# A quantiser's cube taken out of the last tiles' way, and a slot's largest value moved ahead of the late tables

## The chip, the cores and the metric

One core of a Trainium2 chip runs the whole program. It has TensorE (PE, matrix products, with weight loads shown apart as PEld), VectorE (DVE), ScalarE (ACT), GpSimd (POOL, which here also issues all indirect transfers) and SyncE (SP, which issues the direct ones). They meet only through semaphores. The metric is the device time of the program in microseconds (us). The kernel before takes 260.91 us, the median of three runs from 260.31 to 262.14.

## The reference

A sequence of 4 x 512 tokens of width 512 goes through two expert layers, each a residual on a layer norm. `route` stands for the choice of an expert per token:

```python
h = layernorm(x)                                     # layer 1: 4 experts, by token id
x = x + where(route, (silu(h @ C[e].T) * (h @ C[e].T)) @ C[e], 0)

h = layernorm(x)                                     # layer 2: 8 experts, by argmax(h @ router.T)
wq = clip(round(w * s), -1, 1) / s,      s = 1 / clip(mean|w|, 1e-5)
aq = clip(round(a * t), -128, 127) / t,  t = 127 / clip(max|a| over the row, 1e-5)
g, u = aq(h) @ wq(wg[e]).T, aq(h) @ wq(wu[e]).T
r = square(relu(g)) * u
x = x + where(route, aq(r) @ wq(wd[e]).T, 0)
```

All weights of layer 2 become ternary (-1, 0, 1), the activations 8-bit integers. A row's step is t8 = max(1, ratio)/127 in the kernel's scaled units; since r is a square times a linear term, the step enters the second quantiser as its **cube**.

## The kernel before, in words

**Layer 1** handles 19 tiles (B1) of 128 token rows, gathered in order of their expert by POOL's indirect transfer (L468). It goes through the loop over t: PE does two products per tile in split precision (L1484), transposes (L1470), and the router's logits (L1564). DVE writes the result row (L1047, function `residual`), its largest square (L1062, `largest`) and the row's index within its layer-2 expert (L1092, `row_index`). POOL works out the quantiser of the row (`deviation_of`, `roots_of`, `ratio_of`, `cube_of`, L497 to L533), the address (L542, `place`) and stores the 128 rows of 520 columns to DRAM at addresses sorted by expert (L550, `store`). Columns 512 to 519 carry the row's scalars: RSTD, INV, SCALE, NEG, TOKEN, CUBE.

**Layer 2** handles 23 slots (B2) of 128 rows, each of one expert. Slots 0 to 4 (EARLY) are blocks filled by tiles 0 to 14; they are loaded before the last tiles are done. Slots 5 to 22 are late: SP loads them (L391, `load`) once the last three stores have landed and the late tables are there (`slots_ready` at 2). The **late tables** (`late_slots`, `slot_tables`, `slot_factors`, a generator that DVE takes in steps with `next(late)`) say which rows and which expert each slot has: L1108, L1111, L1113, L1117, L1120 (`base`, the row address, signals `slots_ready`), L1125, L1129 (expert), L1137 to L1151 (means of the weights).

A slot takes these steps. DVE quantises the row (L1228, `quantise`), PE transposes it (L1586) and ACT copies it out (L745, qT); PE does the gate and up products (L1592); ACT takes relu and square (L753, L757); DVE multiplies (L1238, `product_of`), takes the largest value (L1248, `largest_product`), its reciprocal and the scale (L1256 and L1262, `product_scale`); ACT quantises the product (L777); PE transposes (L1586), ACT copies (L765), PE does the down product (L1592); DVE adds (L1283, `output`); POOL scatters the rows (L619, `scatter`). POOL also works out out_scale (L609) and, per group of slots, `factors_of`: cap_scale, down_size, least_max (L593 to L596) from the cubes in the loaded rows. `product_scale` waits until the whole group's factors are there (semaphore `sizes`). The late groups are slots 5 to 8, 9 and 10, 11 to 14, 15 to 18, 19 to 22; a group's factors are issued at step u = (first slot - 1), after all its rows have landed.

Every engine runs its instructions in the order written; no planner moves them. In a step u of layer 2 PE does gate(u), up(u), transpose q(u+1), transpose r(u-2), down(u-3); ACT relu and square of u, qT(u+1), rT(u-2), r8(u-1); DVE quantise(u+1), largest and scale of u-1, output(u-4), product(u). In step 4, DVE's quantise(5) stands ahead of product_of(3), and relu2(u) on ACT waits for product_of(u-1), which reads the same tile.

Of the kernel before, what the change touches and what calls it, by code (L numbers as in the profile page):

```python
# [5 lines left out]
ALU = mybir.AluOpType  # L6
ACT = mybir.ActivationFunctionType
X = mybir.AxisListType.X
F32 = mybir.dt.float32
# [4 lines left out]
I32 = mybir.dt.int32  # L14
U32 = mybir.dt.uint32

P = 128
# [20 lines left out]
ROW = D + 8  # L38
RSTD, INV, SCALE, NEG, TOKEN, CUBE = range(D, D + 6)

# [52 lines left out]
def moe_program(nc, x_in, tokens_in, ctx_in, router_in, weights_in, out):  # L93
    with ExitStack() as whole:
# [108 lines left out]
        by_slot = [sb("by_slot0", [P, 2 * EARLY], F32), sb("by_slot1", [P, 3 * (B2 - EARLY)], F32)]  # L203

        masked, late_token = sb("masked", [P, B2 - EARLY], I32), sb("late_token", [P, B2 - EARLY], I32)
        cap_scale, down_size = sb("cap_scale", [P, B2], F32), sb("down_size", [P, B2], F32)
# [133 lines left out]
        def sizes_of(group):  # L340

            return 3 * group

# [68 lines left out]
        def _(pool):  # L412
# [31 lines left out]
            for r in row:  # L444
                pool.memset(r[:, CUBE + 1:], 0.0).then_inc(made, 1)

# [53 lines left out]
            def steps_of(b):  # L500
                roots_of(b)
                ratio_of(b)
                cube_of(b)

            def roots_of(b):
                if not 0 <= b < B1:
                    return
                s, r = ln2[b % 2], row[b % ROWS]
                pool.wait_ge(norm2, 7 * b + 1)
                pool.wait_ge(largest_ready, b + 1)  # L510
                pool.tensor_tensor(r[:, RSTD:INV + 1], s[:, 2:4], half_powers[:, :], ALU.pow).then_inc(norm2, 1)  # L511
                pool.wait_ge(norm2, 7 * b + 3)
                pool.tensor_scalar(r[:, SCALE:SCALE + 1], r[:, INV:INV + 1], r[:, RSTD:RSTD + 1], QMAX,
                                   ALU.min, ALU.mult).then_inc(norm2, 1)

            def ratio_of(b):
                if not 0 <= b < B1:
                    return
                s, r = ln2[b % 2], row[b % ROWS]


                pool.wait_ge(norm2, 7 * b + 3)
                pool.tensor_scalar(s[:, 4:5], r[:, INV:INV + 1], s[:, 3:4], r[:, RSTD:RSTD + 1],
                                   ALU.mult, ALU.mult).then_inc(norm2, 1)

            def cube_of(b):
                if not 0 <= b < B1:
                    return
                s, r = ln2[b % 2], row[b % ROWS]
                pool.wait_ge(norm2, 7 * b + 5)  # L530
                pool.tensor_scalar(s[:, 4:5], s[:, 4:5], 1.0, 1.0 / QMAX, ALU.max, ALU.mult).then_inc(norm2, 1)
                pool.wait_ge(norm2, 7 * b + 6)
                pool.tensor_scalar(r[:, CUBE:CUBE + 1], s[:, 4:5], s[:, 4:5], s[:, 4:5],  # L533
                                   ALU.mult, ALU.mult).then_inc(norm2, 1)
# [10 lines left out]
            def store(b):  # L545
                if not 0 <= b < B1:
                    return
                pool.wait_ge(store_at_ready, b + 1)
                pool.wait_ge(norm2, 7 * b + 7)
                pool.indirect_dma_start(x1_rows, bass.IndirectOffsetOnAxis(ap=store_at[b % ROWS][:, :], axis=0),  # L550
# [18 lines left out]
            for t in range(TICKS):  # L569
                if t >= 2:  # L570
                    gather(t + 3)
                quantising(t - 2)
                place(t - 3)
                if t < B1:
                    store(t - 3)
                if t >= 2:
                    inverse_deviation(t + 2)

            def factors_of(group):
# [9 lines left out]
                if slots[0] == EARLY:  # L589

                    pool.tensor_scalar(masked[:, :], by_slot[1][:, 2 * n:3 * n], token1[:, 0:1], float(MASKED),
                                       ALU.is_ge, ALU.mult).then_inc(masked_ready, 1)
                pool.tensor_tensor(cap_scale[:, few, None], cols_of(slots, CUBE), gu, ALU.mult).then_inc(sizes, 1)  # L593
                pool.tensor_tensor(down_size[:, few, None], cols_of(slots, CUBE), gud, ALU.mult).then_inc(sizes, 1)
                pool.wait_ge(sizes, sizes_of(group - 1) + 1)
                pool.tensor_tensor(least_max[:, few], cap_scale[:, few], minus_one[:, few], ALU.pow).then_inc(sizes, 1)  # L596
                if late:
                    which = slice(slots[0] - EARLY, slots[-1] + 1 - EARLY)
                    pool.wait_ge(masked_ready, 1)
# [235 lines left out]
        def _(dve):  # L835
# [203 lines left out]
            def residual(b):  # L1039
# [3 lines left out]
                if b >= 2:  # L1043
                    dve.wait_ge(norm2, 7 * (b - 1))
                if b >= ROWS:
# [736 lines left out]
```

## Time and profile before

| | |
|---|---|
| profiled execution, time | 260.85 us |
| its span | 258.9 us |
| PE, DVE, ACT, POOL busy | 236.6, 219.7, 210.8, 164.9 us |
| granted TensorE clock, mean | 0.996 of 2.4 GHz |
| DMA | 51.71 MB, 200 GB/s mean |
| layer 1 | about 13 to 176 us |
| layer 2 | about 176 to 252 us |

A row's time is counted from the start of the span; 1.95 us of the execution's time lie outside the span. Busy time of an engine is no bound by itself: what counts is which wait ends last at each place, and whether PE, which has most work, stands still.

### The profile page before, as it was taken

What the parts mean: (1) busy time and instruction counts of PE and PEld (TensorE: products, weight loads), DVE (VectorE), ACT (ScalarE), POOL (GpSimd) and SP (SyncE); (2) the same over time, 40 slices, a digit from 0 to 9 for tenths busy, and PEclk for the clock granted to TensorE, in tenths of its full rate; (3) what the DMA queues carried; (4) which work ended last, traced back from release to release, by engine and by line L of the source; (5) the groups of instructions that cost most, each with busy time, mean ns of one, the idle gap of its engine ahead of it and who ended that gap; (6) DMA issues with size and microseconds to landing.
All of it is one profiled execution on the core that took longest, in us unless ns stands there. A gap on an engine that the chain in (4) does not pass through costs nothing.

```text
span 258.9 us, 5787 instructions
## 1 busy us (share of the span) xinstructions
PE 236.6 (91%) x1410; PEld 172.8 (67%) x1420; DVE 219.7 (85%) x686; ACT 210.8 (81%) x322; POOL 164.9 (64%) x322
## 2 busy tenths in 40 slices
PE   2388999999999999999999999989899999999970
PEld 2235678888888888888888888866355555555530
DVE  5969989979889988898888978869989999999861
ACT  1765799799889888898888888777799999999960
POOL 4463566768866867577676565558728675657553
PEclk9999999999999999999999999999999999999998
DMA  5969972946755599785577534551368962211110
GB/s 194 429 211 389 404 285 86 365 160 237 246 166 159 145 345 406 272 322 146 207 244 228 151 117 161 204 155 57 89 188 273 337 232 83 84 40 67 61 42 0
DMA packets 13726, 51.71 MB, mean 200 GB/s; under 512 B 2750, under 2 KB 2750, under 8 KB 10112
## 3 DMA queue, kind: packets, MB, share of 16 engines
q1 hardware_dynamic: 8816, 37.91, 42.3%
q0 software_dynamic: 4880, 13.44, 14.7%
q8 instruction: 14, 0.23, 0.4%
q14 instruction: 16, 0.13, 0.1%
HBM read 40.49 MB, written 13.48 MB: 208 GB/s over the span
## 4 chain that ended last, share of the span: by engine, by line
PE 79%; DVE 7%; DMA 7%; issue 4%; ACT 1%; POOL 1%; DVEq 0%; POOLq 0%; ACTq 0%
PE bank L1484 38%; PE bank L1592 20%; PE bank L1470 9%; PE bank L1564 6%; DMA staged<-weight_chunks 4%; PE bank L1586 4%; DMA x<-x_rows,gather 2%; PE bank L1503 1%; DVE ctx_lo L933 1%; POOL out_rows L619 1%; DMA token_ids<-token_ids_in 1%; PE bank L1459 1%; DVE at_least L853 1%; DVE stats L991 1%; DVE ternary L899 0%
## 5 line engine op out<-in xcount | busy, mean ns | idle before, releaser
L1592 PE MATMUL bank<-ternary,qT 128*128 x179 | 43.4, 379 | 0.9 <-ACT qT L745 0.5
L665 ACT ACTIVATE ternary<-staged 128x2048 bf16<-128x2048 f32 x20 | 38.0, 1899 | 2.0 <-DMA staged<-weight_chunks 2.0
L671 ACT ACTIVATE ternary<-staged,w_scale 128x1536 int16<-128x1536 f32 x20 | 31.5, 1575 | 2.2 <-DVE w_scale L947 0.6
L1592 PEld LDWEIGHTS bank<-ternary,qT 128*128 128x128 bf16 x184 | 17.7, 97 | 21.4 <-issue 5.9
L550 POOL DMA_INDIRECT x_rows<-row,store_at x19 | 22.2, 1166 | 14.9 <-POOL store_at L542 10.1
L619 POOL DMA_INDIRECT out_rows<-late_rows,late_token x18 | 19.7, 1095 | 16.1 <-DVE late_rows L1283 14.4
L468 POOL DMA_INDIRECT x<-x_rows,gather x16 | 19.1, 1193 | 9.6 <-issue 5.8
L718 ACT ACTIVATE p<-bank,rstd 128x512 f32<-128x512 f32 x19 | 13.0, 685 | 14.2 <-PE bank L1484 14.1
L1592 PE MATMUL bank<-ternary,rT 128*128 x87 | 22.7, 379 | 1.8 <-ACT rT L765 1.5
L1027 DVE SCALAR_TENSOR_TENSOR p<-bank,rstd,p 128x512 f32<-128x512 f32 x19 | 14.2, 749 | 10.5 <-ACT p L718 10.4
L1484 PE MATMUL bank<-ctx_hi,pT_hi 128*128 x76 | 22.4, 416 | 0.3 <-DVE pT_lo L1036 0.3
L1484 PE MATMUL bank<-ctx_hi,hT_hi 128*128 x76 | 22.3, 414 | 0.0
L1484 PE MATMUL bank<-ctx_lo,hT_hi 128*128 x76 | 21.0, 399 | 0.2 <-DVE ctx_lo L933 0.2
L1484 PE MATMUL bank<-ctx_hi,pT_lo 128*128 x76 | 20.8, 395 | 0.0
L1484 PE MATMUL bank<-ctx_lo,pT_hi 128*128 x76 | 20.8, 395 | 0.0
L1564 PEld LDWEIGHTS bank<-router,x1T 128*128 128x128 f32 x152 | 19.7, 191 | 1.5
L1484 PE MATMUL bank<-ctx_hi,hT_lo 128*128 x76 | 20.5, 391 | 0.0
L1564 PE MATMUL bank<-router,x1T 128*128 128x8 f32 x152 | 18.3, 246 | 0.0
L1238 DVE TENSOR_TENSOR prod<-bank,relu 128x512 f32<-128x512 f32 x23 | 15.8, 686 | 1.8 <-ACT relu L757 0.4
L777 ACT ACTIVATE r<-prod,fac 128x512 int16<-128x512 f32 x23 | 16.5, 719 | 0.7 <-DVE fac L1262 0.7
L511 POOL TENSOR_TENSOR row<-ln,half_powers 128x2 f32<-128x2 f32 x19 | 13.8, 725 | 5.0 <-DVE squares L1062 5.0
L1484 PEld LDWEIGHTS bank<-ctx_lo,hT_hi 128*128 128x128 f32 x76 | 14.3, 189 | 3.9 <-issue 0.6
(232 smaller groups left out, 661.9 us busy)
## 6 DMA issues: line engine op xcount, KB each, us to landing
staged<-weight_chunks SPq DMA_DIRECT2D x20, 1024.0 KB, 5.4
late_rows<-x_rows SPq DMA_DIRECT2D x18, 260.0 KB, 3.9
ternary<-ctx_chunks SPq DMA_DIRECT2D x4, 1024.0 KB, 8.2
ternary<-weight_chunks SPq DMA_DIRECT2D x4, 1024.0 KB, 9.4
x_rows<-filler SPq DMA_DIRECT2D x1, 2080.0 KB, 12.8
staged<-x_rows SPq DMA_DIRECT2D x5, 260.0 KB, 3.3
x_rows<-row,store_at POOLq DMA_INDIRECT x19, 5.7
out_rows<-late_rows,late_token POOLq DMA_INDIRECT x18
```

The lines of the kernel that those rows point to most:

```text
L468: pool.indirect_dma_start(x[b % RING], None, x_in, bass.IndirectOffsetOnAxis(ap=gather1[:, b:b + 1], axis=0), bounds_check=N - 1, oob_is_e ...
L550: pool.indirect_dma_start(x1_rows, bass.IndirectOffsetOnAxis(ap=store_at[b % ROWS][:, :], axis=0), row[b % ROWS][:, :], None, bounds_check ...
L619: pool.indirect_dma_start(out, bass.IndirectOffsetOnAxis(ap=token, axis=0), cols_of([b], 0, D), None, bounds_check=N - 1, oob_is_err=False)\
L665: nc.scalar.activation(ternary[:, m * K * D:(m + 1) * K * D], staged_of(i), ACT.Abs, accum_out=abs_sum[:, 2 * i:2 * i + 1]).then_inc(abs_r ...
L671: nc.scalar.activation(ternary[:, m * K * D + DVE_COLS:(m + 1) * K * D].bitcast(I16), staged_of(i)[:, DVE_COLS:], ACT.Copy, scale=w_scale[ ...
L777: nc.scalar.activation(r8[:, :], prod[b % 2][:, :], ACT.Copy, scale=fac[b % 2][:, 2:3])\
L1027: dve.scalar_tensor_tensor(p[:, :], a_ps[b % 2][:, :], rstd1[b % 2][:, :], p[:, :], ALU.mult, ALU.mult).then_inc(p_ready, 1)
L1238: dve.tensor_tensor(prod[b % 2][:, :], u_ps[b % 2][:, :], relu2[:, :], ALU.mult)\
L1470: last = pe.transpose(ps[:, k * P:(k + 1) * P], src[:, k * P:(k + 1) * P], ident[:, :])
L1484: last = pe.matmul(ps[:, :], left[:, k * P:(k + 1) * P], right[:, bass.ds(e * (K * D) + k * D, D)], start=(n == 0 and k == 0), stop=(n == ...
L1564: last = pe.matmul(logits_ps[:, 0:E2], x1T[:, k * P:(k + 1) * P], router[:, k * E2:(k + 1) * E2], start=(k == 0), stop=(k == K - 1))
L1592: last = pe.matmul(ps[:, :], left[:, k * P:(k + 1) * P], ternary[:, bass.ds(e * (3 * K * D) + (kind * K + k) * D, D)], start=(k == 0), sto ...
```

## The change

1. **Cube.** A new column RATIO in each stored row holds the ratio before clamping and cubing. Tiles 0 to 14 (up to EARLY_AFTER) still work out CUBE on POOL ahead of the store; tiles 15 to 18 don't, which takes two POOL instructions out of each. In its place `factors_of` works out, for each of the five late groups, step and cube from the loaded RATIO column: three POOL instructions ahead of cap_scale, each waiting for the one before.
2. **Order of POOL's last tiles.** `roots_of` is split in two (`scale_of` is the new part), and the address and store of tile b-1 are set between the instructions of tile b.
3. **DVE.** `largest_product(1)` and `product_scale(1)` move ahead of one `next(late)`, the step that works out `base` and signals `slots_ready`.
4. **Tiles.** spread, by_slot0, masked, step and cube are put into tiles of the sort at the start (scan, member, earlier, placed), which nothing reads by then.

```diff
-RSTD, INV, SCALE, NEG, TOKEN, CUBE = range(D, D + 6)
+RSTD, INV, SCALE, NEG, TOKEN, CUBE, RATIO = range(D, D + 7)
...
-        spread = sb("spread", [P, 3 * (B2 - EARLY)], F32)
+        spread = scan[:, 0:3 * (B2 - EARLY)]
...
+        step, cube = placed[:, 0:B2 - EARLY], placed[:, 32:32 + B2 - EARLY]
...
-            return 3 * group
+            early = group_of(EARLY) - 1
+            return 3 * min(group, early) + 6 * max(group - early, 0)
+
+        def norm2_at(b):
+
+            return 7 * min(b, EARLY_AFTER + 1) + 5 * max(b - EARLY_AFTER - 1, 0)
...
             def cube_of(b):
-                if not 0 <= b < B1:
+
+                if not 0 <= b <= EARLY_AFTER:
                     return
...
             for t in range(TICKS):
                 if t >= 2:
                     gather(t + 3)
-                quantising(t - 2)
-                place(t - 3)
                 if t < B1:
+                    quantising(t - 2)
+                    place(t - 3)
                     store(t - 3)
...
-                pool.tensor_tensor(cap_scale[:, few, None], cols_of(slots, CUBE), gu, ALU.mult).then_inc(sizes, 1)
-                pool.tensor_tensor(down_size[:, few, None], cols_of(slots, CUBE), gud, ALU.mult).then_inc(sizes, 1)
-                pool.wait_ge(sizes, sizes_of(group - 1) + 1)
+                done = sizes_of(group - 1)
+                cubes = cols_of(slots, CUBE)
+                if late:
+                    which = slice(slots[0] - EARLY, slots[-1] + 1 - EARLY)
+                    pool.tensor_scalar(step[:, which, None], cols_of(slots, RATIO), 1.0, 1.0 / QMAX, ALU.max,
+                                       ALU.mult).then_inc(sizes, 1)
+                    pool.wait_ge(sizes, done + 1)
+                    pool.tensor_tensor(cube[:, which], step[:, which], step[:, which], ALU.mult).then_inc(sizes, 1)
+                    pool.wait_ge(sizes, done + 2)
+                    pool.tensor_tensor(cube[:, which], cube[:, which], step[:, which], ALU.mult).then_inc(sizes, 1)
+                    done += 3
+                    pool.wait_ge(sizes, done)
+                    cubes = cube[:, which, None]
+                pool.tensor_tensor(cap_scale[:, few, None], cubes, gu, ALU.mult).then_inc(sizes, 1)
+                pool.tensor_tensor(down_size[:, few, None], cubes, gud, ALU.mult).then_inc(sizes, 1)
+                pool.wait_ge(sizes, done + 1)
...
+            deviation_of(B1 - 2)
+            roots_of(B1 - 2)
+            place(B1 - 3)
+            scale_of(B1 - 2)
+            ratio_of(B1 - 2)
+            store(B1 - 3)
             deviation_of(B1 - 1)
-            store(B1 - 3)
             place(B1 - 2)
             roots_of(B1 - 1)
             store(B1 - 2)
+            scale_of(B1 - 1)
+            place(B1 - 1)
             ratio_of(B1 - 1)
-            place(B1 - 1)
-            cube_of(B1 - 1)
             store(B1 - 1)
...
             product_of(1)
-            for _ in range(4):
+            for _ in range(3):
                 next(late)
             largest_product(1)
             product_scale(1)
+
+            next(late)
             quantise(4)
```

The first place is on DVE, in the late tables. `fac` holds slot 1's largest value and scale, `base` is what `slots_ready` signals. Before:

```order
L1111 ISA picked,slot_block<-late_reached,late_delta 128x19 [waits chain]
L1111 ISA slot_block 128x1
L1113 TENSOR_TENSOR in_run<-late_reached 128x17
L1117 ISA picked,begins<-in_run,run_last 128x17 [waits chain]
L1117 ISA begins 128x1
L1120 SCALAR_TENSOR_TENSOR base<-slot_block,begins 128x1 [waits chain]
L1125 ISA picked,slot_block<-late_reached,expert_step 128x17
L1125 ISA slot_block 128x1
L1248 TENSOR_REDUCE fac<-prod 128x1 [waits prod_ready]
L1256 RECIPROCAL fac<-fac 128x1 [waits amax_ready]
L1262 TENSOR_SCALAR fac<-fac,cap_scale 128x1 [waits inv_ready,first_sizes]
L1228 TENSOR_SCALAR t_0<-staged 128x512 [waits tT_ready,x1_in4]
```

Now (line numbers are those of the changed file, 32 higher here):

```order
L1143 ISA picked,slot_block<-late_reached,late_delta 128x19 [waits chain]
L1143 ISA slot_block 128x1
L1145 TENSOR_TENSOR in_run<-late_reached 128x17
L1280 TENSOR_REDUCE fac<-prod 128x1 [waits prod_ready]
L1288 RECIPROCAL fac<-fac 128x1 [waits amax_ready]
L1294 TENSOR_SCALAR fac<-fac,cap_scale 128x1 [waits inv_ready,first_sizes]
L1149 ISA picked,begins<-in_run,run_last 128x17 [waits chain]
L1149 ISA begins 128x1
L1152 SCALAR_TENSOR_TENSOR base<-slot_block,begins 128x1 [waits chain]
L1157 ISA picked,slot_block<-late_reached,expert_step 128x17
L1157 ISA slot_block 128x1
L1260 TENSOR_SCALAR t_0<-staged 128x512 [waits tT_ready,x1_in4]
```

The three instructions of the scale of slot 1 now stand ahead of L1117, L1120 and L1125 (L1149, L1152 and L1157 of the changed file); quantise(4) (L1228, L1260 there) is behind all of them in both.

The second place is on POOL, the end of layer 1, with tiles 17 and 18. Before:

```order
L542 TENSOR_SCALAR store_at<-index_f,pad 128x1 [waits index_ready,row_out2]
L511 TENSOR_TENSOR row<-ln_0,half_powers 128x2 [waits largest_ready,norm2]
L513 TENSOR_SCALAR row<-row 128x1 [waits norm2]
L550 DMA x_rows<-row,store_at 17536x520 [waits norm2,store_at_ready]
L523 TENSOR_SCALAR ln_0<-row,ln_0 128x1 [waits norm2]
L542 TENSOR_SCALAR store_at<-index_f,pad 128x1 [waits index_ready,row_out0]
L531 TENSOR_SCALAR ln_0<-ln_0 128x1 [waits norm2]
L533 TENSOR_SCALAR row<-ln_0 128x1 [waits norm2]
L550 DMA x_rows<-row,store_at 17536x520 [waits norm2,store_at_ready]
```

Now (L565 is the store, L557 the address, L520, L527 and L537 root, scale and ratio):

```order
L557 TENSOR_SCALAR store_at<-index_f,pad 128x1 [waits index_ready,row_out2]
L520 TENSOR_TENSOR row<-ln_0,half_powers 128x2 [waits largest_ready,norm2]
L565 DMA x_rows<-row,store_at 17536x520 [waits norm2,store_at_ready]
L527 TENSOR_SCALAR row<-row 128x1 [waits norm2]
L557 TENSOR_SCALAR store_at<-index_f,pad 128x1 [waits index_ready,row_out0]
L537 TENSOR_SCALAR row<-row,ln_0 128x1 [waits norm2]
L565 DMA x_rows<-row,store_at 17536x520 [waits norm2,store_at_ready]
```

The two TENSOR_SCALAR instructions of the cube (L531, L533) are gone from ahead of the last store, and the address comes between the scale and the ratio.

The third place is on POOL, the first late group (slots 5 to 8). Before:

```order
L591 TENSOR_SCALAR masked<-by_slot,token 128x18 [waits x1_in8,x1_in7,by_slot_ready,x1_in6,x1_in5]
L593 TENSOR_TENSOR cap_scale<-late_rows,by_slot 128x4
L594 TENSOR_TENSOR down_size<-late_rows,by_slot 128x4
L596 TENSOR_TENSOR least_max<-cap_scale,minus_one 128x4 [waits sizes]
L600 TENSOR_TENSOR late_token<-late_rows,masked 128x4 [waits masked_ready]
```

Now (the name `earlier` is the tile that holds masked, `placed` the one that holds step and cube):

```order
L606 TENSOR_SCALAR earlier<-by_slot,token 128x18 [waits x1_in8,x1_in7,by_slot_ready,x1_in6,x1_in5]
L612 TENSOR_SCALAR placed<-late_rows 128x4
L615 TENSOR_TENSOR placed<-placed 128x4 [waits sizes]
L617 TENSOR_TENSOR placed<-placed 128x4 [waits sizes]
L621 TENSOR_TENSOR cap_scale<-placed,by_slot 128x4 [waits sizes]
L622 TENSOR_TENSOR down_size<-placed,by_slot 128x4
L624 TENSOR_TENSOR least_max<-cap_scale,minus_one 128x4 [waits sizes]
L627 TENSOR_TENSOR late_token<-late_rows,earlier 128x4 [waits masked_ready]
```

Three instructions in a chain of waits have come in ahead of cap_scale. The other four late groups have the same three.

## Rows read from the trace of the kernel before

**Rows 1.** The page, part 1: busy us, share of the span, instructions

```profile
PE 236.6 (91%) x1410; PEld 172.8 (67%) x1420; DVE 219.7 (85%) x686; ACT 210.8 (81%) x322; POOL 164.9 (64%) x322
```

**Rows 2.** Chain of waits in order of time: start us, us, what, from 192 us on

```profile
192.19 2.65 PE bank L1592 x12
...
243.95 2.59 PE bank L1592 x12
```

**Rows 3.** Timeline of PE: start us, us, engine, line, op, out<-in, [idle before<-releaser]

```profile
187.67 0.40 PE L1586 MATMUL bank<-ident,t 128*128 128x128 bf16 x4 [0.41 <-DVE t L1228]
...
189.69 1.90 PE L1592 MATMUL bank<-ternary,qT 128*128 x8 [0.46 <-ACT qT L745]
...
200.75 0.39 PE L1586 MATMUL bank<-ident,t 128*128 128x128 bf16 x4
```

**Rows 4.** Timeline of DVE, 185 to 190.5 us, tables and second slot

```profile
185.03 0.41 DVE L1111 CUSTOM_DVE_ANT_0 picked<-late_reached,late_delta 128x19 f32<-128x19 f32 x1
...
185.57 0.18 DVE L1117 CUSTOM_DVE_ANT_0 picked<-in_run,run_last 128x17 f32<-128x17 f32 x1
...
185.79 0.16 DVE L1120 SCALAR_TENSOR_TENSOR base<-slot_block,begins 128x1 int32<-128x1 f32 x1
...
185.97 0.68 DVE L1248 TENSOR_REDUCE fac<-prod 128x1 f32<-128x512 f32 x1
...
186.95 0.21 DVE L1262 TENSOR_SCALAR fac<-fac,cap_scale 128x1 f32<-128x1 f32 x1
...
187.08 0.54 DVE L1228 TENSOR_SCALAR t<-staged 128x512 int16<-128x512 f32 x1
...
187.60 0.68 DVE L1238 TENSOR_TENSOR prod<-bank,relu 128x512 f32<-128x512 f32 x1
...
190.45 0.55 DVE L1228 TENSOR_SCALAR t<-late_rows 128x512 int16<-128x512 f32 x1 [0.43 <-DMA late_rows<-x_rows]
```

**Rows 5.** Timeline of ACT, 187 to 190 us

```profile
187.19 0.72 ACT L777 ACTIVATE r<-prod,fac 128x512 int16<-128x512 f32 x1 [0.68 <-DVE fac L1262]
...
188.43 0.63 ACT L757 ACTIVATE relu<-relu 128x512 f32<-128x512 f32 x1
...
188.97 0.58 ACT L745 ACTIVATE qT<-bank 128x512 bf16<-128x512 int16 x1
```

**Rows 6.** Timeline of POOL, 182.9 to 185.8 us: cube and store of tile 18

```profile
182.93 0.22 POOL L531 TENSOR_SCALAR ln<-ln 128x1 f32<-128x1 f32 x1
...
183.26 0.58 POOL L533 TENSOR_SCALAR row<-ln 128x1 f32<-128x1 f32 x1
...
184.71 1.08 POOL L550 DMA_INDIRECT x_rows<-row,store_at  x1 [0.86 <-POOL row L533]
```

**Rows 7.** The same store (L550, 184.5 to 186 us): time from issue to landing

```profile
DMA to landing us min/median/max: 2.2/2.2/2.2
```

**Rows 8.** Timeline of SP, 182 to 189 us: loads of slots 5 and 6

```profile
187.81 1.45 SPq L391 DMA_DIRECT2D late_rows<-x_rows  x2
```

**Rows 9.** Timeline of POOL, 196 to 198.3 us: factors of slots 5 to 8

```profile
196.23 0.39 POOL L591 TENSOR_SCALAR masked<-by_slot,token 128x18 int32<-128x18 f32 x1 [0.72 <-DMA late_rows<-x_rows]
...
196.69 0.20 POOL L593 TENSOR_TENSOR cap_scale<-late_rows,by_slot 128x4 f32<-128x4 f32 x1
...
197.00 1.27 POOL L596 TENSOR_TENSOR least_max<-cap_scale,minus_one 128x4 f32<-128x4 f32 x1
```

**Rows 10.** Timeline of DVE, 198 to 200 us: scale of slot 5, quantising of slot 8

```profile
198.00 0.16 DVE L1256 RECIPROCAL fac<-fac 128x1 f32<-128x1 f32 x1
...
198.31 0.21 DVE L1262 TENSOR_SCALAR fac<-fac,cap_scale 128x1 f32<-128x1 f32 x1
...
199.69 0.62 DVE L1228 TENSOR_SCALAR t<-late_rows 128x512 int16<-128x512 f32 x1
```

**Rows 11.** Timeline of POOL, 207 to 208 us: slots 9 and 10

```profile
207.21 0.73 POOL L596 TENSOR_TENSOR least_max<-cap_scale,minus_one 128x2 f32<-128x2 f32 x1
```

**Rows 12.** Timeline of DVE, 209 to 210 us: scale of slot 9

```profile
209.67 0.21 DVE L1262 TENSOR_SCALAR fac<-fac,cap_scale 128x1 f32<-128x1 f32 x1
```

More of the change, by code:

```diff
@@ L199, in moe_program @@
         slot_means = [sb("slot_means0", [P, 2], F32), sb("slot_means1", [P, 3], F32)]
-        spread = sb("spread", [P, 3 * (B2 - EARLY)], F32)
-        by_slot = [sb("by_slot0", [P, 2 * EARLY], F32), sb("by_slot1", [P, 3 * (B2 - EARLY)], F32)]
-        masked, late_token = sb("masked", [P, B2 - EARLY], I32), sb("late_token", [P, B2 - EARLY], I32)
+        spread = scan[:, 0:3 * (B2 - EARLY)]
+        by_slot = [member[:, 0:2 * EARLY], sb("by_slot1", [P, 3 * (B2 - EARLY)], F32)]
+        masked, late_token = earlier[:, 0:B2 - EARLY].bitcast(I32), sb("late_token", [P, B2 - EARLY], I32)
+        step, cube = placed[:, 0:B2 - EARLY], placed[:, 32:32 + B2 - EARLY]
         cap_scale, down_size = sb("cap_scale", [P, B2], F32), sb("down_size", [P, B2], F32)
@@ L501, in steps_of @@
                 roots_of(b)
+                scale_of(b)
                 ratio_of(b)
@@ L508, in roots_of, with scale_of @@
                 s, r = ln2[b % 2], row[b % ROWS]
-                pool.wait_ge(norm2, 7 * b + 1)
+                pool.wait_ge(norm2, norm2_at(b) + 1)
                 pool.wait_ge(largest_ready, b + 1)
                 pool.tensor_tensor(r[:, RSTD:INV + 1], s[:, 2:4], half_powers[:, :], ALU.pow).then_inc(norm2, 1)
-                pool.wait_ge(norm2, 7 * b + 3)
+            def scale_of(b):
+                if not 0 <= b < B1:
+                    return
+                r = row[b % ROWS]
+                pool.wait_ge(norm2, norm2_at(b) + 3)
                 pool.tensor_scalar(r[:, SCALE:SCALE + 1], r[:, INV:INV + 1], r[:, RSTD:RSTD + 1], QMAX,
@@ L519, in ratio_of @@
                 s, r = ln2[b % 2], row[b % ROWS]
-                pool.wait_ge(norm2, 7 * b + 3)
-                pool.tensor_scalar(s[:, 4:5], r[:, INV:INV + 1], s[:, 3:4], r[:, RSTD:RSTD + 1],
+                pool.wait_ge(norm2, norm2_at(b) + 3)
+                pool.tensor_scalar(r[:, RATIO:RATIO + 1], r[:, INV:INV + 1], s[:, 3:4], r[:, RSTD:RSTD + 1],
                                    ALU.mult, ALU.mult).then_inc(norm2, 1)
             def cube_of(b):
-                if not 0 <= b < B1:
+                if not 0 <= b <= EARLY_AFTER:
                     return
                 s, r = ln2[b % 2], row[b % ROWS]
-                pool.wait_ge(norm2, 7 * b + 5)
-                pool.tensor_scalar(s[:, 4:5], s[:, 4:5], 1.0, 1.0 / QMAX, ALU.max, ALU.mult).then_inc(norm2, 1)
-                pool.wait_ge(norm2, 7 * b + 6)
+                pool.wait_ge(norm2, norm2_at(b) + 5)
+                pool.tensor_scalar(s[:, 4:5], r[:, RATIO:RATIO + 1], 1.0, 1.0 / QMAX, ALU.max, ALU.mult).then_inc(norm2, 1)
+                pool.wait_ge(norm2, norm2_at(b) + 6)
                 pool.tensor_scalar(r[:, CUBE:CUBE + 1], s[:, 4:5], s[:, 4:5], s[:, 4:5],
```

7 lines of the change are left out of this document (3 added, 4 removed).

## The prediction

> **What bounds the kernel now.** I read four views in this order. The page says that PE has the most work, 236.6 us of the 258.9 [rows 1], but DVE and ACT are near it, so the question is where PE stands still. The chain of waits answers that: from 192.19 us to the piece that starts at 243.95 us it runs along PE's products alone [rows 2]. So a microsecond that PE gains or loses at 190 us stays in the total, unless PE is stopped again later; work saved behind 192 us on another engine is worth nothing. Third, PE's own timeline shows two stops just before that stretch: 0.41 us before the transpose at 187.67 us (for quantise(4) on DVE), and 0.46 us before gate(4) at 189.69 us (for qT(4) on ACT) [rows 3]. Fourth, I followed these stops back on ACT, DVE, POOL and SP. gate(4) needs qT(4) at 188.97 us, which is behind relu2(3) at 188.43 us, behind relu(3), behind r8(1) at 187.19 us, which waited 0.68 us for the scale of slot 1 [rows 5]. That scale ends at 186.95 + 0.21 us on DVE, with three table instructions of 185.57 to 185.97 us ahead of it [rows 4]. So the moved max sits on the path; the late rows are a second path that joins it, since quantise(5) waited 0.43 us for its rows, until 190.45 us [rows 4].
>
> **The change, part by part.**
>
> *Slot 1's scale ahead of base (DVE).* The scale is reached earlier by 185.97 - 185.57 = 0.40 us [rows 4]. This alone would bring gate(4) forward by at most the 0.46 us of its stop. But quantise(4) and product_of(2) stand behind the same instructions in either order, and relu2(3) reads what product_of(2) must have read first: that product ends at 187.60 + 0.68 = 188.28 us, and relu2(3) starts at 188.43 us [rows 4, 5]. What shortens DVE's sequence is only that L1117 no longer waits for the instruction just before it: 185.57 - 185.03 us covers L1111 and L1113 and one such wait, and L1117 to L1120 has another, 0.22 us for a 0.18 us instruction [rows 4]. I take 0.11 us saved from the first. The Trainium skill, VectorE: DVE Perf Modes, section "The DRAIN you can't avoid", says of chained Vector instructions that the semaphore costs nothing extra; by that the reordering would save DVE nothing and gate(4) would move only by what relu2(3) waits beyond product_of(2). A second saving is possible: L1111 took 0.41 us where the like L1117 took 0.18 us, and POOL's store was being issued beside it, from 184.71 us for 1.08 us [rows 4, 6]. That store now comes earlier, so 0 to 0.23 us more. The Trainium skill, SBUF — State Buffer, section "Who interferes with whom", has a Vector instruction with two SBUF inputs contend with GpSimd instructions that read SBUF, which fits this row; by the rule the 0.23 us goes fully. I take half, as one row is thin evidence. Together gate(4) comes 0.18 us (relu2(3) then starts at 188.25 us) to 0.41 us earlier, 0.3 us taken.
>
> *The last stores (POOL).* Without the cube the store of tile 18 is ready when the ratio is. Its two instructions start at 182.93 and 183.26 us and the last ends at 183.84 us [rows 6], 0.91 us. The new order also puts store 17 in front of the scale of tile 18 and the address (which can't come before row_index(18)) beside it. Chained from the same pieces I get a start of the last store at about 182.8 us in place of 184.71 us, 1.9 us earlier; its landing, 2.2 us after the issue [rows 6, 7], goes from 186.91 to about 185.0 us. The bounds are 0.9 us (only the cube) and 2.0 us.
>
> *What the earlier stores buy (SP).* The load of slot 5 starts at 187.81 us [rows 8], 0.90 us after that landing. It needs the landings and `slots_ready`, which is L1120's end, 185.95 us before [rows 4]. Now the tables are late: L1120 moves behind the scale, by the three scale instructions, 187.08 - 185.97 = 1.11 us, less the wait saved: 186.95 us, or 186.72 us without the disturbance of L1111. So the wait changes its name from the stores to the tables, and load 5 can start at 186.72 + 0.91 = 187.63 us at best. At worst SP then has five semaphores and a register to read where it had two and the register. No row prices a wait that is already met; with up to 0.1 us for each of three, and 186.95 us, that is 188.2 us. I take 187.9 us, 0.1 us later than before, nearer the rows that I have. The gain of 1.9 us on POOL is thus lost whole. quantise(5), product_of(3), relu2(4) and qT(5) follow the rows' landing, and gate(5) before had no slack on that path: PE's gain of 0.3 us at gate(4) is given back at gate(5), and the sum there is +0.1 us (-0.2 to +0.4).
>
> *Three instructions more per late group (POOL).* In the first group POOL waited until 196.23 us for the rows of slot 8, the last of its group; cap_scale starts 0.46 us on, least_max at 197.00 us and ends at 198.27 us [rows 9]. DVE's scale of slot 5 starts at 198.31 us, behind a reciprocal that ended at 198.16 us [rows 10]: it begins right when least_max is done. I take it that there is no slack, so what the new chain takes, DVE waits. Price: a TENSOR_SCALAR with constants and a dependent one behind it start 183.26 - 182.93 = 0.33 us apart [rows 6]; a TENSOR_TENSOR and its dependent, L593 to L596, 197.00 - 196.69 = 0.31 us with an independent one between [rows 9]. 0.33 + 2 x 0.31 = 0.95 us. The bounds are 0.45 us (three at the 0.15 us of independent ones) and 1.45 us (the L533 of 0.58 us as measure for all three). With the rows landing 0.1 us later, the scale of slot 5 comes 0.95 + 0.1 = 1.05 us late.
>
> Behind it on DVE, in order, are output(2), product_of(6) and quantise(8). quantise(8) ran from 199.69 us for 0.62 us, to 200.31 us [rows 10], and PE took its transpose at 200.75 us [rows 3]: 0.44 us of slack. So PE stops for 1.05 - 0.44 = 0.6 us, measured against its old time, which already holds the +0.1 us from above. ACT's copy for gate(8) then follows 0.5 us after the transpose has begun and is in time behind down(4). From there PE is the bound again and carries the 0.6 us to the end; a slot takes (243.95 - 192.19)/17 = 3.04 us of PE [rows 2], and DVE, which kept its slack of 0.44 us over these slots, has less to do in one.
>
> *The other four groups.* For slots 9 and 10 least_max ends at 207.21 + 0.73 = 207.94 us and slot 9's scale starts at 209.67 us [rows 11, 12]: 1.73 us of slack for 0.95 us. The last three groups issue their factors the same two steps ahead of use, so they cost nothing either. If this cover were gone each would cost up to 0.95 us.
>
> *Layer 1.* Tiles 0 to 14 have the same seven POOL instructions. Tiles 15 and 16 have two fewer, but their stores wait for the address from DVE. Nothing on PE waits for them: nothing gained. The move of tiles into those of the sort, and one column less to clear: nothing.
>
> **The sum** against the profiled execution's 260.85 us: 260.85 + 0.6 = 261.5 us, rounded. The profiled execution stands 0.06 us under the median of 260.91 us, so the sum holds for the median too.
>
> **The rivals.**
>
> *The chain is hidden.* If the three instructions cost near 0.45 us and load 5 starts at its best, the scale of slot 5 comes 0.3 us late, inside the 0.44 us. Then gate(4)'s gain remains to the extent that the load allows it: -0.2 to -0.4 us, 260.5 us. For it: POOL's spans are rough, and least_max's 1.27 us was long. Against it: the coincidence of 198.27 and 198.31 us.
>
> *Both joints fail, more than I took.* Load at 188.2 us, chain of 1.45 us: the scale is 1.85 us late, PE stops 1.4 us: 262.3 us.
>
> *POOL becomes the bound in layer 2.* If each late group stopped DVE as the first does, by 0.95 us, five times, it would be 260.85 + 4.75 = 265.6 us, slower by 1.8%. This decides once a group's factors come later than their slack, 1.73 us in the second. Against it: 1.73 us is near twice the price.
>
> *The change frees the loads.* Were the stores alone what load 5 waits for, it would start up to 1.0 us earlier (the tables were ready at 185.95 us). Against it: L1120 moves behind the scale, and the load needs it. It would give -0.4 us (the stop at gate(4) gone) and take 1 us off the group's start, so that the chain is hidden too: 260.4 us. It falls together with the first rival in time.
>
> **How the numbers follow.** My forecast has 0.55, the chain hidden or the loads freed 0.27, both joints worse 0.15, POOL as the bound 0.02; 0.01 is left for a gain beyond 1% that no row shows. The range takes the hidden case and the worse one, and the 0.3 us or so by which medians of this kernel move: 260.2 to 262.4 us. About 1%, 2.6 us, is what a measurement of this kernel can tell from no change. Every case but the fourth lies inside it: faster by over 1% 0.01, within 1% 0.96, slower 0.03.
>
> **What the changed profile would show.** The scale of slot 1 should start at about 186.4 us, L1120's successor end at 186.7 to 187.0 us, the last store start at about 182.8 us, load 5 at 187.6 to 188.2 us with SP's last wait on DVE and not on a store. The first late group's masked should start near 196.3 us, least_max end near 199.3 us, and DVE should idle about 1 us ahead of slot 5's scale with POOL as the releaser; PE should stop at the transpose for slot 8, by 0.6 us, and nowhere else after 192 us. If DVE doesn't idle there, the chain was hidden and I am wrong by that step; if load 5 starts before 187.5 us, the step on SP is wrong.

## The result, and the profile after

The changed kernel takes 259.89 us, the median of 22 runs (258.76 to 260.99), beside 261.17 us for the kernel before in the same rounds (22 runs, 260.22 to 262.95): ratio 0.9945, interval 0.9928 to 0.9962, 1.4 us less by the ratio and 1.3 us by the medians. The prediction of 261.5 us (260.2 to 262.4) missed it, in size and in direction. The profiled execution took 259.56 us with a span of 257.6 us.

Busy times on the page are within 0.4 us of those of [rows 1], but for POOL's, which is 1.7 us less:

```profile
PE 236.3 (92%) x1420; PEld 172.8 (67%) x1420; DVE 219.3 (85%) x686; ACT 210.8 (82%) x322; POOL 163.2 (63%) x329
```

The chain of waits (start us, us, what) again runs along PE's products to the end, as in [rows 2]:

```profile
190.48 2.71 PE bank L1625 x12
...
242.66 2.59 PE bank L1625 x12
```

The last piece is 1.29 us earlier than its like in [rows 2]. Most of that shows in DVE's timeline at the residual of tiles 6 and 17, in layer 1. Before:

```profile
82.44 0.67 DVE L1047 SCALAR_TENSOR_TENSOR row<-bank,x 128x512 f32<-128x512 f32 x1
...
169.20 0.69 DVE L1047 SCALAR_TENSOR_TENSOR row<-bank,x 128x512 f32<-128x512 f32 x1 [1.01 <-PE bank L1484]
```

After:

```profile
82.05 0.67 DVE L1079 SCALAR_TENSOR_TENSOR row<-bank,x 128x512 f32<-128x512 f32 x1
...
167.89 0.69 DVE L1079 SCALAR_TENSOR_TENSOR row<-bank,x 128x512 f32<-128x512 f32 x1 [0.98 <-PE bank L1517]
```

From tile 6 to tile 17 it is 86.76 us before and 85.84 us after: 0.92 us for 11 tiles, 0.084 us in each, mostly ahead of the instructions whose order the change moved. PE never idles in this stretch. Its products there multiply h or p, split into a high and a low half, by the context matrix ctx, split in the same way; ctx is the operand that PE streams, and h or p is loaded as the weights. These are the groups by form (line, engine, op, out<-in, count, busy us, mean ns, idle us) between 66 and 160 us; counts under 48 are records that the trace lacks. Before:

```profile
L1484 PE MATMUL bank<-ctx_hi,hT_hi 128*128 x48 | 14.0, 413 | 0.0
L1484 PE MATMUL bank<-ctx_lo,hT_hi 128*128 x48 | 13.2, 398 | 0.0
L1484 PE MATMUL bank<-ctx_hi,hT_lo 128*128 x48 | 13.0, 391 | 0.0
L1484 PE MATMUL bank<-ctx_lo,pT_hi 128*128 x47 | 12.9, 395 | 0.0
L1484 PE MATMUL bank<-ctx_hi,pT_lo 128*128 x44 | 12.0, 394 | 0.0
```

After:

```profile
L1517 PE MATMUL bank<-ctx_hi,hT_hi 128*128 x48 | 14.0, 414 | 0.0
L1517 PE MATMUL bank<-ctx_lo,pT_hi 128*128 x48 | 13.0, 392 | 0.0
L1517 PE MATMUL bank<-ctx_hi,pT_lo 128*128 x48 | 12.9, 391 | 0.0
L1517 PE MATMUL bank<-ctx_lo,hT_hi 128*128 x48 | 12.8, 389 | 0.0
L1517 PE MATMUL bank<-ctx_hi,hT_lo 128*128 x48 | 12.8, 389 | 0.0
```

PE's instructions are the same. The four forms with a low half last 9, 3, 3 and 2 ns less each (398 to 389, 395 to 392, 394 to 391, 391 to 389); the two with both high halves change by 1 ns at most (413 to 414 for the one shown). Four of each per tile make 68 ns of the 84. So PE's own rate in layer 1 rose.

In layer 2 PE's timeline answers to [rows 3]. The 0.41 us stop ahead of the transpose for slot 4 (186.00 us) is at most 0.1 us now, the one ahead of gate(4) (187.95 us) is as long as before, and a new one of 0.23 us stands ahead of the transpose for slot 9:

```profile
186.00 0.40 PE L1619 MATMUL bank<-ident,t 128*128 128x128 bf16 x4
...
187.95 1.90 PE L1625 MATMUL bank<-ternary,qT 128*128 x8 [0.47 <-ACT qT L777]
...
199.14 0.39 PE L1619 MATMUL bank<-ident,t 128*128 128x128 bf16 x4
...
202.57 0.38 PE L1619 MATMUL bank<-ident,t 128*128 128x128 bf16 x4 [0.23 <-issue]
```

DVE and ACT (compare [rows 4, 5, 10]): on DVE the first table instruction, slot 1's scale, base, quantise(5), slot 5's scale and quantise(8); on ACT relu2(3), which now waits for product_of(2), and the copy qT(4).

```profile
183.67 0.18 DVE L1143 CUSTOM_DVE_ANT_0 picked<-late_reached,late_delta 128x19 f32<-128x19 f32 x1
...
184.84 0.21 DVE L1294 TENSOR_SCALAR fac<-fac,cap_scale 128x1 f32<-128x1 f32 x1
...
185.18 0.21 DVE L1152 SCALAR_TENSOR_TENSOR base<-slot_block,begins 128x1 int32<-128x1 f32 x1
...
188.80 0.55 DVE L1260 TENSOR_SCALAR t<-late_rows 128x512 int16<-128x512 f32 x1 [0.45 <-DMA late_rows<-x_rows]
...
196.96 0.21 DVE L1294 TENSOR_SCALAR fac<-fac,cap_scale 128x1 f32<-128x1 f32 x1 [0.44 <-POOL least_max L624]
...
198.34 0.63 DVE L1260 TENSOR_SCALAR t<-late_rows 128x512 int16<-128x512 f32 x1
```

```profile
186.70 0.63 ACT L789 ACTIVATE relu<-relu 128x512 f32<-128x512 f32 x1 [0.40 <-DVE prod L1270]
...
187.23 0.58 ACT L777 ACTIVATE qT<-bank 128x512 bf16<-128x512 int16 x1
```

POOL and SP ([rows 6, 8, 9]): on POOL the last store, then the first late group from its first instruction to least_max (L612 is the first of the new chain of three); on SP the loads from slot 5 on, and its waits between 180 and 190 us (us in total, times, longest):

```profile
181.89 1.09 POOL L565 DMA_INDIRECT x_rows<-row,store_at  x1 [0.87 <-DVE fac L1280]
...
193.96 0.39 POOL L606 TENSOR_SCALAR earlier<-by_slot,token 128x18 int32<-128x18 f32 x1
...
194.43 0.26 POOL L612 TENSOR_SCALAR placed<-late_rows 128x4 f32<-128x4 f32 x1
...
195.88 1.04 POOL L624 TENSOR_TENSOR least_max<-cap_scale,minus_one 128x4 f32<-128x4 f32 x1
```

```profile
186.14 2.52 SPq L399 DMA_DIRECT2D late_rows<-x_rows  x3
```

```profile
SPq L413 <- DMA x_rows<-row,store_at: 3.8, 1, 3.8
SPq L398 <- DVE base L1152: 1.2, 1, 1.2
```

The load of slot 8, from issue to landing, before (SP's L391, 191 to 192 us) and after (L399, 189.3 to 190 us):

```profile
DMA to landing us min/median/max: 4.8/4.8/4.8
```

```profile
DMA to landing us min/median/max: 3.4/3.4/3.4
```

Since the whole stretch is shifted by layer 1, I count from quantise(3), here before (183.26 us) and after (181.90 us):

```profile
183.26 0.54 DVE L1228 TENSOR_SCALAR t<-staged 128x512 int16<-128x512 f32 x1
```

```profile
181.90 0.54 DVE L1260 TENSOR_SCALAR t<-staged 128x512 int16<-128x512 f32 x1
```

From there (times with a plus sign are counted so from here on), gate(4) went from +6.43 to +6.05 us, the last store from +1.45 to -0.01, load 5 from +4.55 to +4.24, the scale of slot 5 from +15.05 to +15.06, and the transpose for slot 22 on PE from +60.08 to +60.15. Layer 2 gained 0.38 us at gate(4), still had 0.25 us of it at the transpose for slot 8 (+17.50 before, +17.25 after), and had lost it all by the transpose for slot 9 (+20.61 before, +20.67 after).

### The profile page after: what moved, and what is told of

Read it like the earlier page. It is cut to its first block, busy times and chain, and to the rows that moved or that the text cites. A ratio compares the mean times of both kernels' runs of the same rounds, so it can differ in the third digit from the quotient of the medians.

```text
span 257.6 us, 5804 instructions
## 1 busy us (share of the span) xinstructions
PE 236.3 (92%) x1420; PEld 172.8 (67%) x1420; DVE 219.3 (85%) x686; ACT 210.8 (82%) x322; POOL 163.2 (63%) x329
## 4 chain that ended last, share of the span: by engine, by line
PE 74%; DVE 12%; ACT 5%; issue 4%; DMA 3%; POOL 1%; DVEq 0%; ACTq 0%; POOLq 0%
PE bank L1517 33%; PE bank L1625 20%; PE bank L1503 8%; PE bank L1597 5%; PE bank L1619 4%; DMA ternary<-weight_chunks 3%; PE bank L1715 2%; DVE ctx_lo L965 1%; DVE p L1059 1%; DVE ternary L931 1%; PE bank L1536 1%; ACT ternary L697 1%; DVE pT_lo L1068 1%; POOL out_rows L646 1%; DVE prod L1270 1%
## 5 line engine op out<-in xcount | busy, mean ns | idle before, releaser
L1625 PE MATMUL bank<-ternary,qT 128*128 x184 | 44.0, 379 | 0.8 <-ACT qT L777 0.5
L565 POOL DMA_INDIRECT x_rows<-row,store_at x19 | 22.8, 1201 | 14.8 <-POOL store_at L557 9.3
L1625 PE MATMUL bank<-ternary,rT 128*128 x92 | 23.6, 379 | 1.5 <-ACT rT L797 1.5
L1517 PE MATMUL bank<-ctx_lo,hT_hi 128*128 x76 | 20.4, 390 | 0.2 <-DVE ctx_lo L965 0.2
L520 POOL TENSOR_TENSOR row<-ln,half_powers 128x2 f32<-128x2 f32 x19 | 13.8, 728 | 5.0 <-DVE squares L1094 5.0
L785 ACT ACTIVATE relu<-bank 128x512 f32<-128x512 f32 x23 | 13.7, 596 | 3.6 <-PE bank L1625 2.7
```

Of the source, the lines that this page charges most:

```text
L1517: last = pe.matmul(ps[:, :], left[:, k * P:(k + 1) * P], right[:, bass.ds(e * (K * D) + k * D, D)], start=(n == 0 and k == 0), stop=(n == ...
L1625: last = pe.matmul(ps[:, :], left[:, k * P:(k + 1) * P], ternary[:, bass.ds(e * (3 * K * D) + (kind * K + k) * D, D)], start=(k == 0), sto ...
```

## The experiments

**The place of the tiles.** The four tiles that the change puts into others took 384 bytes a partition, so h, hT_lo, ctx_hi, ctx_lo and all behind them start 384 bytes lower. First the two kernels crossed:

```diff
 # layout_only: the kernel before with
-        spread = sb("spread", [P, 3 * (B2 - EARLY)], F32)
+        spread = scan[:, 0:3 * (B2 - EARLY)]
 # and by_slot0, masked likewise
```

> The kernel before, with one thing changed: the four small tiles put into tiles of the sort, so that all tiles behind them in SBUF (h, hT_lo, the two context halves, qT and the rest) start 384 bytes lower; order and number of instructions are those of before. Theory A (the place of the tiles sets the speed of PE's layer-1 products): residual to residual from tile 6 to tile 17 takes 85.8 us as in the changed kernel, not 86.8 us as before, and the time falls by about 1.0 us, ratio about 0.996. Theory B (the new order of POOL's instructions, or the ratio written into the row, makes layer 1 faster): 86.8 us and ratio 1.000.

```diff
 # after_padded: the changed kernel with
+        pads = [sb("pad0", [P, 3 * (B2 - EARLY)], F32), sb("pad1_", [P, 2 * EARLY], F32), sb("pad2", [P, B2 - EARLY], I32)]
```

> The changed kernel with three unused tiles of 224, 64 and 96 bytes a partition in front of the others, so that h, the context halves and all behind them are at the addresses of the kernel before; instructions unchanged. Theory A: tile 6 to tile 17 takes 86.8 us again, and what is left of the gain is that of the second slot and the late loads, 0 to 0.4 us, ratio 0.9985 to 1.000. Theory B: 85.8 us, ratio about 0.9945.

DVE's timeline at tiles 6 and 17, layout_only:

```profile
82.80 0.67 DVE L1047 SCALAR_TENSOR_TENSOR row<-bank,x 128x512 f32<-128x512 f32 x1
...
168.64 0.69 DVE L1047 SCALAR_TENSOR_TENSOR row<-bank,x 128x512 f32<-128x512 f32 x1 [0.97 <-PE bank L1484]
```

after_padded:

```profile
83.50 0.67 DVE L1080 SCALAR_TENSOR_TENSOR row<-bank,x 128x512 f32<-128x512 f32 x1
...
170.27 0.69 DVE L1080 SCALAR_TENSOR_TENSOR row<-bank,x 128x512 f32<-128x512 f32 x1 [1.02 <-PE bank L1518]
```

85.84 and 86.77 us: theory A holds to 0.01 us of the two kernels, and theory B falls. The times: layout_only 0.9968 (0.9947 to 0.9989), 0.8 us less than before; after_padded 0.9972 (0.9950 to 0.9993), 0.7 us less. The second gained more than I expected, and more than its trace shows behind residual 17 (83.35 us to the last output against 83.54 us before). Its interval reaches down to 0.2 us, and its profiled execution, 261.73 us, was the slowest of its twelve, so the trace can't tell where the rest of the 0.7 us lies.

Then single places. The five whose names begin with ctx ran once each, so only their traces count, not their times. All are the changed kernel with unused bytes in the inner block of tiles; in the last one it is the kernel before.

```diff
             stack.append(inner)
+            space = sb("space", [P, 96], F32)     # 384 bytes; 32: 128, 16: 64, 64: 256 bytes
             h = sb("h", [P, D], F32)
             hT_lo = sb("hT_lo", [P, D], F32R)
             # ctx_alone_128: 128 bytes here instead
             ctx_hi = sb("ctx_hi", [P, E1 * K * D], F32R)
```

> The changed kernel with 384 unused bytes ahead of h, hT_lo and the two context halves alone, which puts these four back at their addresses of before; all other tiles stay where the change has them. Theory A1 (it is the place of the context halves, which PE streams through in its products, or of hT_lo): tile 6 to tile 17 takes 86.8 us. Theory A2 (it is the place of the small tiles, or of something that ACT, DVE or POOL touch beside PE): 85.8 us.

> The same with 128 unused bytes: ctx_hi then starts at byte 163,328 of a partition, between the slow place (163,584) and the fast one (163,200); 163,584 and 163,328 are multiples of 256, 163,200 is not. Theory A1a (multiples of 256 are slow): tile 6 to 17 takes 86.8 us. Theory A1b (the speed depends on a coarser place, such as which bytes two reads share at once): 85.8 us or something between.

> The changed kernel with 128 unused bytes between hT_lo and ctx_hi: only the two context halves (ctx_hi at byte 163,328, ctx_lo at 196,096, both multiples of 256) leave their places, h and hT_lo keep the fast ones. Theory A1 (the operand that PE streams sets the speed): tile 6 to 17 takes 86.8 us. Rival (hT_lo or h, which were moved along so far): 85.8 us.

> The changed kernel with 64 unused bytes ahead of h, hT_lo and the context halves: ctx_hi starts at byte 163,264, 192 past a multiple of 256. Theory A1a (only multiples of 256 are slow): 85.8 us from tile 6 to tile 17. Rival (128 past a multiple of 256 is the one good place, as in the changed kernel): 86.3 to 86.8 us.

> The changed kernel with 256 unused bytes ahead of the same four tiles: ctx_hi starts at byte 163,456, 128 past a multiple of 256, as in the changed kernel (163,200) and 256 higher. Theory A1a or any rule that repeats every 256 bytes: 85.8 us. Rival (the lower the place, the faster, or a boundary between 163,200 and 163,328): 86.8 us.

> The kernel before with 128 unused bytes ahead of h, hT_lo and the context halves, and nothing else: no tile shares another's place, no instruction differs. ctx_hi starts at byte 163,712, 128 past a multiple of 256 and higher than any place so far. If the place alone accounts for the faster layer 1 (a rule that repeats every 256 bytes): tile 6 to 17 in 85.8 us, and a time about 0.9 us under the kernel before, ratio 0.9955 to 0.9975. If what helped in the changed kernel was putting tiles into those of the sort, or a lower place: 86.8 us and ratio 1.000.

| kernel | ctx_hi at byte | past a multiple of 256 | tile 6 to 17, us |
|---|---|---|---|
| before, move_only, after_padded | 163,584 | 0 | 86.76, 86.77, 86.77 |
| ctx_up_384 | 163,584 | 0 | 86.76 |
| ctx_up_128 | 163,328 | 0 | 86.74 |
| ctx_alone_128 | 163,328 | 0 | 86.67 |
| ctx_up_64 | 163,264 | 192 | 86.15 |
| ctx_up_256 | 163,456 | 128 | 85.83 |
| before_up_128 | 163,712 | 128 | 85.82 |
| after, layout_only and four more | 163,200 | 128 | 85.83 to 85.85 |

The rows of before_up_128 and of ctx_alone_128:

```profile
82.63 0.67 DVE L1048 SCALAR_TENSOR_TENSOR row<-bank,x 128x512 f32<-128x512 f32 x1
...
168.45 0.69 DVE L1048 SCALAR_TENSOR_TENSOR row<-bank,x 128x512 f32<-128x512 f32 x1 [0.97 <-PE bank L1485]
```

```profile
82.94 0.67 DVE L1080 SCALAR_TENSOR_TENSOR row<-bank,x 128x512 f32<-128x512 f32 x1
...
169.61 0.69 DVE L1080 SCALAR_TENSOR_TENSOR row<-bank,x 128x512 f32<-128x512 f32 x1 [1.02 <-PE bank L1518]
```

So it is the operand that PE streams, the context halves; the low half lies 32,768 bytes behind, at the same remainder. Theory A1a holds in its main part, not wholly: 192 gave 86.15 us, between the two, where A1a had 85.8 us. It isn't a mere half-way case either: the form ctx_hi,hT_hi took 417 ns there, against 413 and 414 ns at the other two remainders, while ctx_lo,hT_hi took 393 ns, between 398 and 389 ns. Lower or higher, and what lies in the tiles of the sort, make no difference. before_up_128 alone, with one unused tile, is faster than the kernel before, 0.9972 (0.9956 to 0.9988), 260.19 against 260.95 us.

**The move on DVE.**

```diff
 # move_only: the kernel before with the diff's last hunk
 # after_tables_first: the changed kernel without it
```

> The kernel before with the move on DVE alone (largest value and scale of slot 1 ahead of base). No change of addresses, POOL as before. Tile 6 to 17: 86.8 us by both theories. The stores still land at 186.9 us, base at 187.0 us, so load 5 stays within 0.2 us; gate(4) 0.1 to 0.2 us earlier, given back at gate(5). Ratio 0.999 to 1.001.

Time 0.9987 (0.9970 to 1.0004). gate(4) is at +6.29 us, 0.14 us earlier; load 5 is at +4.56 us, as before, and DVE's quantise(5) at +7.24 against +7.19 us: given back as expected.

> The changed kernel with the largest value of slot 1 back behind the late tables' base; cube and stores as changed. If the move is what gave 0.3 to 0.45 us at gate(4), PE's gate(4) now starts that much later against quantise(3), but load 5 comes earlier than in the changed kernel, by up to 1 us, since base is ready earlier; the first group's factors then come earlier and DVE idles less than the 0.44 us it idled for slot 5. Prediction: within 0.3 us of the changed kernel either way, ratio to before 0.994 to 0.997.

259.34 us, 0.9935 (0.9915 to 0.9956), the lowest ratio of all but not apart from the changed kernel's. gate(4) is at +6.20 us, 0.15 us behind the changed kernel's, where 0.3 to 0.45 us was expected: with move_only's 0.14 us it says that DVE's move gave some 0.15 us of the 0.38 us at gate(4), and the earlier stores the other 0.23 us. Load 5 is at +3.22 us, 1.02 us ahead of it, as the expectation had it; the scale of slot 5 at +14.61 us. I had expected DVE to idle less there than 0.44 us. It idled the same, as DVE itself came 0.45 us sooner:

```profile
196.99 0.21 DVE L1294 TENSOR_SCALAR fac<-fac,cap_scale 128x1 f32<-128x1 f32 x1 [0.45 <-POOL least_max L624]
```

**The chain of three.**

```diff
 # cube_in_layer1: the changed kernel with
-                if not 0 <= b <= EARLY_AFTER:
+                if not 0 <= b < B1:
 # cube_of(17) and cube_of(18) ahead of the last stores, and the three instructions of step and cube left out of factors_of
 # tables_first_two_groups: after_tables_first with
-GROUPS = [..., range(EARLY, FULL), range(9, 11), ...]
+GROUPS = [..., range(EARLY, 7), range(7, FULL), range(9, 11), ...]
```

> The changed kernel with the cube of the last four tiles back on POOL ahead of their stores and without the three instructions in front of each late group's factors; new order of the stores, DVE's move and addresses as changed. Theory C (the chain of three is what takes the 0.38 us of gate(4) away again): least_max of the first group ends about 1.0 us earlier, DVE doesn't idle 0.44 us for slot 5, and from quantise(3) to quantise(22) it takes 58.1 us, not 58.4 us; the last store comes 0.9 us later, which base hides. Ratio to the changed kernel 0.999. Rival: the loads decide, and it takes 58.4 us all the same.

> The changed kernel with slot 1's scale back behind the tables and the first late group cut in two (slots 5, 6 and 7, 8). Load 5 at 185.6 us as without the cut, factors of slot 5 and 6 ready without waiting for the rows of slots 7 and 8. Theory C: DVE never idles for slot 5's scale, PE never stops for slot 8 or 9; from quantise(3) to quantise(22) 57.9 to 58.1 us against 58.2 us (tables first alone) and 58.4 us (the change). If that stretch stays at 58.2 us, PE's stop lies elsewhere.

> The changed kernel with slot 1's scale behind the tables again and the cube of the last four tiles back in layer 1 (no chain of three in the late groups); the new order of the stores and the new addresses stay. The last store is 0.9 us later than in the changed kernel, which its landing shows: load 5 waits for the store again. Expected: from quantise(3) to the transpose for slot 22 on PE 59.7 to 60.0 us, where the changed kernel takes 60.15 us; time 259.4 to 259.9 us, ratio to before 0.9935 to 0.9955. If the time is not under the changed kernel's beyond noise, there is nothing left to win in the order of layer 2's start, and the gate(4) stop of 0.46 us is all that the tables and the stores can give back.

The group's work in POOL's timeline, from the first row's start to least_max's end, took 2.04 us before, 2.96 us in the changed kernel, 1.81 us in cube_in_layer1. The 2.04 us is the exception: the other kernels without the chain all take 1.80 to 1.82 us, since their least_max lasts 1.04 or 1.05 us as in the changed kernel, not 1.27 us as in the trace before. So the chain costs 2.96 - 1.81 = 1.15 us. Without the chain DVE doesn't idle for slot 5's scale (+14.68 us), and quantise(22) is at +58.23 us against +58.40 us; 58.1 us was expected. 0.9952 (0.9933 to 0.9970), no different from the changed kernel. With two groups the scale comes at +14.29 us, DVE doesn't idle for it, and yet quantise(22) is at +58.65 us, a plain miss: PE stopped once, for which the profile names no releaser (the transposes for slots 9 and 10 are 3.70 us apart in place of 3.04 us):

```profile
205.89 0.38 PE L1617 MATMUL bank<-ident,t 128*128 128x128 bf16 x4 [0.49 <-issue]
```

Time 0.9967 (0.9947 to 0.9988). tables_first_cube_in_layer1 missed in the same way: the transposes for slots 7 and 8 are 3.65 us apart, the one for slot 22 is at +60.35 us, the time 260.52 us, 0.9982 (0.9962 to 1.0002); load 5 is at +4.16 us.

## Why the prediction was wrong, point by point

**The move of tiles: "nothing gained" was the step that failed.** I costed it by instructions and waits, and it has none. It moved the operand that PE streams, and in a stretch that is PE alone that gave 0.92 us between tiles 6 and 17. layout_only and before_up_128 have it without the rest, after_padded, ctx_up_384 and ctx_alone_128 lose it with the rest in place. That is shown. In the trace it is two thirds of the 1.4 us; by the times, the place alone gave 0.8 and 0.7 us (layout_only, before_up_128). Some more may lie ahead of tile 6: residual 0 to 6 took 47.98 to 48.48 us in the six kernels at remainder 0 and 47.81 to 48.00 us in the eight at 128, 0.24 us less in the mean, but with a scatter of 0.5 and 0.2 us within the two groups.

**Slot 1's scale: right.** 0.3 us taken for gate(4), 0.38 us measured, inside the 0.18 to 0.41 us. relu2(3) became the one that waits, 0.40 us for product_of(2), as the prediction had it. L1111's 0.41 us became 0.18 us (L1143) once the store was gone from its side, and the whole 0.23 us came where I had taken half. The Trainium skill, SBUF — State Buffer, section "Who interferes with whom", has a Vector instruction with two SBUF inputs contend with a GpSimd instruction that reads SBUF. The traces agree in part: the instruction took 0.41 us in the four kernels where the store had started 0.32 us ahead, and 0.18 us in cube_in_layer1 beside a store that had started 0.73 us ahead and was still being issued. Why the second store cost nothing, no run here tells. From L1113 (L1145) to quantise(4) it is 1.64 us after 1.71 us: the wait taken out of DVE's sequence saved 0.07 us, where I took 0.11 us.

**The last store: 1.9 us taken, 1.46 us measured.** Scale, address and ratio of tile 18 start at 180.10, 180.41 and 180.70 us, behind the store of tile 17, and the store of tile 18 starts 0.86 us after the ratio's end. The prediction doesn't give the starts that it chained, so which of these pieces it had 0.4 us too short can't be said. For the load it made no odds, since that then waited for base.

**Load 5: the wait changed its name as predicted** (SP waited 1.2 us for base), **but the time did not.** From base's end, 185.39 us, to the load it took 0.75 us, where I had put 0.90 us after a landing and more semaphores. With the 0.23 us of L1111, load 5 came 0.31 us earlier, not 0.1 us later, and gate(5) kept most of its gain: the transpose for slot 6 behind it starts at +11.18 us after +11.42 us.

**The chain of three: the price was 0.2 us short, the slack was not nothing, and the group's start was wrong.** 0.95 us taken, 1.15 us measured. Against the trace before it comes out as 2.96 - 2.04 = 0.92 us, but only because least_max lasted 1.27 us in that one trace. The same long least_max, and a landing of slot 8 that was later than in the other three kernels with the old stores, made the slack nothing there. In those three, slot 5's scale stands at +15.01 to +15.06 us as before, but least_max ends 0.33 us (layout_only), 0.43 us (before_up_128) and 0.57 us (move_only) ahead of it. For layout_only:

```profile
196.39 1.04 POOL L596 TENSOR_TENSOR least_max<-cap_scale,minus_one 128x4 f32<-128x4 f32 x1
```

```profile
197.76 0.21 DVE L1262 TENSOR_SCALAR fac<-fac,cap_scale 128x1 f32<-128x1 f32 x1
```

The coincidence of 198.27 and 198.31 us, on which the forecast rested, was thus that of one trace. And the group started at +12.06 us, not +12.97 us: slot 8's rows landed 3.4 us after their issue and not 4.8 us, and POOL took the group straight behind its scatter. I had shifted the old landing along. So least_max ended at +15.02 us as in the trace before, the scale of slot 5 came no later, DVE idled 0.44 us in place of 1 us, and PE did not stop for slot 8.

**The other four late groups: right.** Their least_max ends 0.83 to 0.86 us ahead of the scale that needs it, where it had 1.73 to 1.96 us before, and DVE idles no more there than it did.

**PE did stop, one slot on.** 0.23 us ahead of 202.57 us, put down to "issue". Between the transposes for slots 8 and 9 there are 3.12 us before and 3.43 us after, and 3.04 us where nothing stops. This took back what was left of gate(4)'s gain. It isn't the change's doing in any way that I can show: seven kernels with the same layer 2 (the changed one and its six with other places) had the transpose for slot 22 between +59.80 and +60.35 us, three with the old one at +60.06 to +60.20 us. What PE waits for there stays open.

**In sum**, by the two traces: from residual 17 to the last output the change gave 0.0 us where I had +0.6 us, and up to residual 17 it gave -1.3 us where I had none: the 0.92 us shown, and 0.39 us ahead of tile 6, which lies within the scatter of the start (residual 6 starts between 81.99 and 83.50 us in the fifteen traces). The times don't split quite so. The place alone is worth 0.7 to 0.8 us, and the rest of the change with the old place 0.7 us (0.2 to 1.3; after_padded). What that second part is, beyond 0.2 us seen in its trace, stays open.

## What to carry to other kernels

A change that allocates, drops or shares a tile moves everything allocated behind it, and can change the speed of an engine that no instruction of the diff touches: compare one period of a stretch that the diff leaves alone before explaining the rest, and fix the addresses by padding when timing an order. Where one engine is the bound, try its streamed operand at a few offsets; here 128 unused bytes were worth 0.3%. A transfer's time from issue to landing is not a constant: slot 8's load changed from 4.8 to 3.4 us with the order around it, so don't carry such a time along. And before a forecast rests on a slack of nothing, read it in a second trace: here one long instruction of 1.27 us in place of 1.04 us hid a slack of 0.3 to 0.6 us.

## What the runs showed of the hardware that was not expected

- PE's products in split precision, 512 columns of a 4-byte operand: the four forms with a low half run at 389 to 392 ns where the streamed operand's tile starts 128 bytes past a multiple of 256, and at 391 to 398 ns where it starts on one; those with both high halves run at 413 to 415 ns in both. With 192 the stretch lies between. A tile of layer 1 takes 7.80 against 7.89 us (85.84 and 86.76 us over 11). 64 past wasn't tried, and why the remainder matters isn't known.
- The load of slot 8 took 3.1 to 3.4 us to land with the new order of the stores and DVE's move, 4.2 us with the tables first (3.5 us with the cube in layer 1 too), 4.5 to 4.8 us with the old stores, in the traces that show its landing. Why isn't known.
- Between the transposes for slots 7 and 10 PE loses time in most traces, by up to 0.66 us, with no releaser. Seven kernels with the same layer 2 differ by 0.55 us at the transpose for slot 22, more than the 0.38 us that the edits gained at gate(4).
- A chain of three 128x4 instructions on POOL, each waiting for the one before, put least_max 1.15 us later: they start 0.3 us apart, and cap_scale behind them lasts 0.46 us in place of 0.20 us.
